# Matrix products that walk their moving operand and their output from the last column to the first

## The reference

```python
def cond(x, side, embed, stage):                       # 32 sequences of 256 tokens, 256 features, float32
    q = x + embed[stage][..., None]
    attn = softmax(einsum('bsd,btd->bst', q, side), axis=-1)
    return einsum('bst,btd->bsd', attn, side)

def ffn(x, ...):                                       # 8 experts of rank 16, 2 of them per token, 1024 hidden
    t = x * rsqrt(mean(x * x, -1) + 1e-6) * norm_w
    weights = top2_normalised(softmax(t @ gate_w.T))
    h1 = t @ w1.T + 2 * (t @ a1[e].T) @ b1[e].T        # for each expert e
    h3 = t @ w3.T + 2 * (t @ a3[e].T) @ b3[e].T
    act = silu(h1) * h3
    out_e = act @ w2.T + 2 * (act @ a2[e].T) @ b2[e].T
    return sum_e weights[:, e] * out_e

return x + ffn(cond(x, side, ...))
```

## Time and profile before

| | us |
|---|---|
| median of 3 runs | 1308.93 (1307.21 to 1309.12) |
| the profiled execution, own time | 1308.66 |
| its span, first to last instruction | 1306.9 |
| TensorE busy | 1301.1 |
| weight loads busy (beside TensorE) | 1139.3 |
| VectorE busy | 843.5 |
| ScalarE busy | 527.5 |
| GpSimd busy | 249.9 |

### The profile page before, as it was taken

One profiled execution on the slowest core, in us unless ns is written; L12 is line 12 of the kernel. 1 busy time (PEld: TensorE's weight loads), 2 busy tenths in 40 slices (PEclk: granted clock), 3 DMA queues, 4 the chain that ended last, 5 costly groups with the idle time before them and its releaser, 6 DMA issues.

```text
span 1306.9 us, 18607 instructions
## 1 busy us (share of the span) xinstructions
PE 1301.1 (100%) x7286; PEld 1139.3 (87%) x7286; DVE 843.5 (65%) x1558; ACT 527.5 (40%) x991; POOL 249.9 (19%) x213
## 2 busy tenths in 40 slices
PE   9999999999999999999999999999999999999998
PEld 8999998888888888888888888888888888888887
DVE  6776656756665576656675667557675666565556
ACT  6776753333343344333333334333333343243332
POOL 3556540202011020202020202011020202020200
PEclk9999999999999999999999999999999999999999
DMA  9555810020202020201102020202020101102000
GB/s 294 145 147 154 233 43 33 2 73 2 73 2 73 1 73 1 59 16 33 42 2 73 1 73 2 73 1 74 2 73 1 57 17 35 40 1 73 1 17 17
DMA packets 71791, 69.56 MB, mean 53 GB/s; under 512 B 7050, under 2 KB 62744, under 8 KB 71576
## 3 DMA queue, kind: packets, MB, share of 16 engines
q1 hardware_dynamic: 71392, 68.37, 17.5%
q10 hardware_dynamic: 312, 0.02, 0.0%
HBM read 51.27 MB, written 17.10 MB: 52 GB/s over the span
## 4 chain that ended last, share of the span: by engine, by line
PE 98%; ACT 1%; DVE 0%; issue 0%; DVEq 0%
PE bank L1205 31%; PE bank L1204 31%; PE bank L1206 30%; PE bank L1330 2%; PE bank L1257 2%; PE bank L1308 1%; PE bank L1250 1%; ACT prob L663 0%; PE bank L1216 0%; ACT qT_hi L646 0%; ACT kT_hi L647 0%; DVE probT_lo L886 0%; DVE x_out L1148 0%; PE bank L1295 0%; ACT value_hi L657 0%
## 5 line engine op out<-in xcount | busy, mean ns | idle before, releaser
L1076 DVE TENSOR_TENSOR act_a<-silu_a,bank 128x512 f32<-128x512 f32 x128 | 87.7, 686 | 210.9 <-PE bank L1206 194.2
L754 ACT ACTIVATE br_hi<-act_br 128x512 fp32r<-128x512 f32 x128 | 81.0, 633 | 188.6 <-DVE act_br L1087 188.6
L747 ACT ACTIVATE silu_b<-bank 128x512 f32<-128x512 f32 x128 | 76.3, 596 | 187.9 <-PE bank L1206 187.0
L590 POOL TENSOR_TENSOR t_lo<-t_in,t_hi 128x512 fp32r<-128x512 f32 x32 | 40.6, 1291 | 552.2 <-ACT t_hi L734 552.2
L1205 PE MATMUL bank<-w2T_lo,s_hi 128*128 128x256 f32 x512 | 144.7, 283 | 0.0
L1206 PE MATMUL bank<-w2T_hi,s_lo 128*128 128x256 f32 x512 | 143.3, 280 | 0.0
L1204 PE MATMUL bank<-w2T_hi,s_hi 128*128 128x256 f32 x512 | 142.7, 279 | 0.0
L1084 DVE TENSOR_TENSOR act_b<-silu_b,bank 128x512 f32<-128x512 f32 x128 | 88.0, 688 | 81.4 <-PE bank L1206 80.4
L743 ACT ACTIVATE silu_a<-bank 128x512 f32<-128x512 f32 x128 | 75.8, 592 | 134.1 <-PE bank L1206 134.0
L609 POOL TENSOR_TENSOR v_lo<-v_full,v_hi 128x512 fp32r<-128x512 f32 x64 | 94.5, 1508 | 136.6 <-ACT v_hi L739 136.6
L1097 DVE TENSOR_TENSOR br_lo<-act_br,br_hi 128x512 fp32r<-128x512 f32 x128 | 104.7, 818 | 5.6 <-ACT br_hi L754 3.1
(11 more groups left out here) (197 smaller groups left out, 3242.2 us busy)
## 6 DMA issues: line engine op xcount, KB each, us to landing
kv<-in_fside_BxSxS SPq DMA_DIRECT2D x32, 256.0 KB, 3.3
x_in<-in_x SPq DMA_DIRECT2D x32, 256.0 KB, 4.0
t_scratch<-oT SPq DMA_DIRECT2D x32, 256.0 KB, 2.5
t_in<-t_scratch SPq DMA_DIRECT2D x16, 512.0 KB
x_out<-in_x SPq DMA_DIRECT2D x16, 512.0 KB, 4.0
out<-x_out SPq DMA_DIRECT2D x30, 256.0 KB, 4.0
rho<-scale_scratch SPq DMA_DIRECT2D x16, 256.0 KB
rstd<-scale_scratch SPq DMA_DIRECT2D x16, 256.0 KB
```

The source lines that it names most:

```text
L747: nc.scalar.activation(silu_b[:, :], h1_bank[j % 2][:, :], ACT.Silu).then_inc(silu_b_ready, 1)
L754: nc.scalar.activation(br_hi[j % 2][:, :], act_br[j % 2][:, :], ACT.Copy).then_inc(br_hi_ready, 1)
L1076: nc.vector.tensor_tensor(act_a[j % 2][:, :], silu_a[j % 2][:, :], h3_bank[j % 2][:, :], ALU.mult).then_inc(act_a_ready, 1)
```

## The change

`product` turns its output and both parts of its moving operand round before it issues the three matmuls: the address begins at the last column and the step is -1 element. The weights are not turned. Since output and moving operand turn together, each column of the result lands where it did. Every product of both stages goes through this function: scores, attend, low_rank, first_expert, second_expert, down_y, down_z and finish_y. Single matmuls that are not written through `product` (the first scores, the gate, the transposes and three of `last_down_z`) stay as they are. The order of the instructions on every engine is the same before and after.

```diff
             def product(dst, w, x_parts, start, stop, grouped=True):
 
                 (w_hi, w_lo), (x_hi, x_lo) = w, x_parts
+                dst, x_hi, x_lo = dst[:, ::-1], x_hi[:, ::-1], x_lo[:, ::-1]
                 nc.tensor.matmul(dst, w_hi, x_hi, start=start, stop=False, skip_group_check=not grouped)
                 nc.tensor.matmul(dst, w_hi, x_lo, start=False, stop=False, skip_group_check=not grouped)
                 return nc.tensor.matmul(dst, w_lo, x_hi, start=False, stop=stop, skip_group_check=not grouped)
```

## The result

The changed kernel takes 1333.3 us, the median of four runs (1331.76 to 1333.52), against 1308.95 for the kernel before (four runs, 1307.21 to 1309.12). The ratio is 1.0187, interval [1.0169, 1.0204]: slower by 1.9%, where no change was forecast. The profiled execution took 1331.76 us, with a span of 1330.0; before it was 1308.66 and 1306.9, so the span grew by 23.1 us.

The account below looks back on a forecast made before the run. The prediction took TensorE, full with the matmuls of `product`, to bound the kernel. Its terms summed as 1308.7 + 0 (long matmuls) + 0 (short ones) = 1308.7 us, range 1255 to 1380 us.

Parts of the forecast that it names:

- no change: Whole kernel: long matmuls stay within 0.4 ns of 226.8, time 1306 to 1311 us; chance 0.34, the single likeliest.
- What bounds the kernel: TensorE, busy 1301.1 of 1306.9 us; each nanosecond on a product matmul is paid one for one by the end.
- The moving operand of the long matmuls: Reading 512 columns from the last, in 4029 matmuls of `product`: 0 ns each, between bounds of 215.6 and 436 ns.
- The excess: Time over one column per cycle in `product`: 13.5 ns per long matmul, 10.9 per short one, 81.5 us in all.
- The short ones: 2484 matmuls of 256 columns: taken at 0, forms only exchanging places, with bounds of -18.9 and +6.0 us.
- The output: Downward write into the bank: no wait moves; its cost shows only together with the read's, within the same bounds.
- The mixture in the last tile: Three matmuls that stay ascending after turned ones, 0.7 us in all: mixing directions costed at nothing.
- A second excess: Each of the 6513 matmuls pays its extra cycles twice: 66.5 us more, 1375 us; chance 0.12.
- Fewer collisions: Weight load and moving stream both walk downwards and collide less: up to 66.5 us saved, 1242 us; chance 0.22.
- Half rate: Neighbouring columns join into one access only when ascending: long matmuls 436 ns, 2401 us; chance 0.11.
- Only the short ones dealt anew: Only 256-column steps shift: 1290 us at best, 1315 at worst; chance 0.10 for faster, 0.11 for slower.

Follow-up runs that it names:

- e14_still: Kernel before, with the moving operand reading its first column 512 or 256 times (step 0), output written as before: 1249.5 us.
- e1_read: Kernel before, with only the moving operand read backwards and the output written upwards: 1332.8 us, ratio 1.0187.
- e13_inner: Kernel before, with moving operand and output walking blocks of 16 columns in order, downwards inside each block: 1500.2 us.
- e7_64: Kernel before, nothing turned, with the products of 512 columns loading only 64 columns of weights: 1319.9 us.
- e10_8: Kernel before, nothing turned, with the products of 512 columns loading only 8 columns of weights: 1310.4 us.
- e2_write: Kernel before, with only the output written backwards and the moving operand read upwards: 1308.7 us, ratio 1.0003.
- e11_8_down: Changed kernel, with the products of 512 columns loading only 8 columns of weights: 1331.5 us.
- e4_one_col_down: Changed kernel, with every weight load of a product reading its first column 128 times: 1332.1 us, ratio 1.0182.
- e17_short: Kernel before, with only the products of 256 columns turned, moving operand and output: 1307.6 us, ratio 0.9989.
- e18_short_middle: Kernel before, with only the second matmul of each 256-column product turned, moving operand and output: 1305.4 us, ratio 0.9975.
- e19_alternate: Kernel before, with every other 256-column matmul turned through the whole program, all long ones upwards: 1308.87 us, ratio 0.9997.

## Why the prediction was wrong, point by point

**What bounds the kernel: right.** TensorE's chain carried every nanosecond to the end: +24.8 us in the long steps, -1.7 at the start, +23.1 in the span. The long matmuls, named as those that carry everything, carried it.

**The moving operand of the long matmuls, taken at 0 ns: this step failed.** The reason given was that "a price that does not ask where the operands lie has no evident reason to ask in which direction they are walked". The first half is true and the second doesn't follow from it. Where the operands begin matters little (the same 226.7 and 233.3 ns for t with w1 and for v with b3), but the order of the columns within one operand does: 226.7, 233.3 and 266.7 ns for the same columns. The excess was in plain sight in the earlier trace rows, and its cause was looked for in a meeting with the weight load and hardly in the stream's own walk. e14_still shows what it is, the walk through the memory, 13.5 ns upwards and 2.5 for a stream that stands still. An excess that comes of the walk has every reason to change with the walk. e1_read gives the missing term: 6.6 ns on a long matmul for reading backwards, +24.8 us over all of them. Why this order costs more is not shown by any run.

**The short ones, taken at 0: right in size (300.9 to 300.8 us).** The reason, that forms exchange their places, fits: the fourth of each six matmuls of w2T went from 113.8 to 118.0 ns while their mean stayed at 118.2, and b2T went from 118.0 to 117.0 in the piece. The bounds of -18.9 and +6.0 us were read off rounding: rows that print 10 ns show 0.11 and 0.12 by turns for any step near 117.6. To the nanosecond the 24 steps of the earlier trace rows run from 113 to 120.

Why the backward walk costs the short ones nothing can only be argued. Half a long step, 113.3 ns upwards and 116.7 downwards, lies under the 117.8 that the short ones take anyway, so something else could hold them and hide the walk. In e13_inner half a long step is 133.3, above that, and the short steps rose, to 131.2. But a floor at 117.8 that has nothing to do with the stream doesn't fit e14_still, where they fell to 111.7. A candidate is the weight load, whose duration goes with its columns. Here it is in the groups by form for 128 columns (before), 64 (e7_64) and 8 (e10_8); the last two numbers are the mean of one in ns and the idle time before them in us:

```profile
L1204 PEld LDWEIGHTS bank<-t_hi,w1T_hi 128*128 128x128 f32 x256 | 48.1, 188 | 8.9
L1206 PEld LDWEIGHTS bank<-t_hi,w1T_hi 128*64 128x64 f32 x256 | 34.4, 134 | 21.7
L1206 PEld LDWEIGHTS bank<-t_hi,w1T_hi 128*8 128x8 f32 x256 | 22.6, 88 | 31.2
```

188, 134 and 88 ns are 0.83 ns a column, so by this estimate the columns of a whole load take some 107 ns, near a short step. No run gave the short products a smaller load, so it is not shown.

**The output, taken with the read: right that it costs nothing**, e2_write 1.0003.

**The mixture in the last tile, at nothing: right.** Timeline of the changed kernel, where three unturned matmuls follow turned ones, as in the earlier trace rows:

```profile
1321.31 0.40 PE L1427 MATMUL bank<-s_hi,a2T_hi 128*128 128x512 f32 x1
1321.54 0.39 PE L1428 MATMUL bank<-s_hi,a2T_lo 128*128 128x512 f32 x1
1321.78 0.39 PE L1430 MATMUL bank<-s_lo,a2T_hi 128*128 128x512 f32 x1
1322.00 0.28 PE L1205 MATMUL bank<-w2T_hi,s_hi 128*128 128x256 f32 x1
```

They take 0.69 us, 0.01 more than before.

**The rivals.** *A second excess* named the right kind of thing and the right place, extra cycles on each long matmul by the order of the read, and its sign. Its size was off: 16 cycles (6.6 ns) came and not 27 (11.2 ns), and nothing on the short ones instead of 8.6 ns, so 24 us instead of 66.5. What I held against it, "neither way is favoured", was an absence in the trace and no evidence. *Fewer collisions*, the one I gave the most after no change, falls with e10_8 and e11_8_down: with a sixteenth of the columns to load neither direction's step moves. In e4_one_col_down the load has no direction at all, and the backward stream still takes 233.3 ns. *Half rate* would have been 436 ns; even the worst order tried, e13_inner, takes 266.7. *Only the short ones dealt anew* came true without a price: the steps changed places, and the whole stayed within 0.2% by e17_short.

**Open.** Why the upward walk is the cheaper one; whether the output's order has a share in what turned blocks cost; between 16 and 128 columns, where turned blocks begin to cost; why the upward excess is the same 32 cycles at 384 and at 512; why 64 or one repeated weight column lengthen the upward step and 8 don't; why e18_short_middle gains and e19_alternate doesn't. Other block sizes and other mixtures were not tried.

## What to carry to other kernels

When TensorE is the bound, read the step from start to start and ask of each excess over a column per cycle what it hangs on, before costing an edit that touches it; an unexplained excess has no price of 0 under a change of the access order. In long matmuls let the moving operand walk upwards, or in large pieces that do (blocks of 128 were free), and look twice at nested patterns with small backward pieces, which cost 18% of a step here (read and output in that order together). The plain direction of the output costs nothing, so a reversal that is needed belongs there.

## What the runs showed of the hardware that I had not expected

- A moving operand of 512 fp32r columns takes 215.8 ns standing still, 226.7 upwards, 233.3 downwards and, with its output in the same order, 266.7 downwards in blocks of 16; a short one of 256 columns between 111.7 and 131.2.
- Consecutive reads within a line of 16 bytes go at full rate and each crossing to another pays (the Trainium skill, SBUF — State Buffer, the note on lines in the section "Door 1: The DMA port swizzle"). e14_still, which never leaves its line, agrees, with 2.5 ns of excess left; e1_read crosses the same lines as the kernel before, in the opposite order, and pays 6.6 ns more, which that rule doesn't tell apart.
- The pattern of the weight load can lengthen an upward stream (230.1 ns beside 64 columns, 231.2 beside a repeated one, 226.7 beside 8 or 128); a downward one stayed at 233.3 to 233.4 beside the same four loads. Beside the repeated column two of three upward steps were 233 or 234 ns, about the downward step.
- Turning the second of three short matmuls took 1.9 ns off each step of w2T and 0.25% off the kernel (0.9975 [0.9966, 0.9985]); turning all of them took 0.11% off (0.9989), every other one nothing (0.9997).
